# Routing two batches of the third group, instead of one, beside a half output projection

## What is computed

```python
x = x + tanh(g_xattn) * xattn(layernorm(x), ctx)        # 16 heads, latent dims, rope
n = layernorm(x).reshape(16 * 112, 512)
logits = n @ gate_w.T                                   # 64 experts
topv, topi = top_k(logits, 8)
W = zeros(N, 64).at[rows, topi].set(softmax(topv))
out = sum over experts e of (silu(gate_e(n)) * up_e(n)) * W[:, e] @ dp_w[e].T
out = out + sigmoid(n @ sh_gate1_w.T) * shared_mlp(n)
x = x + tanh(g_ffn) * out
```

## Time and profile before

| what | us |
|---|---|
| three executions | 1713.53, 1716.02, 1720.42 |
| median | 1716.02 |
| profiled execution, its own time | 1701.07 |
| its span, first to last instruction | 1699.2 |
| PE busy in the span | 1475.1 |
| DVE busy | 1138.6 |
| POOL busy | 994.1 |
| turning phase with routing of group 2 (g = 3) | 120.10 |
| half output pass, first transpose to last product | 996.24 to 1022.53 |

### The profile page before, as it was taken

The page is one execution under the profiler, slowest core; times in us unless marked ns, Lnnn a source line. Parts: engine busy times, 40 slices in busy tenths (PEclk is TensorE's granted clock), DMA queues, the critical chain, the costliest instruction groups (busy, mean ns, idle before and its releaser), DMA issues. The chain is left out here.

```text
span 1699.2 us, 24951 instructions
## 1 busy us (share of the span) xinstructions
PE 1475.1 (87%) x7674; PEld 1194.8 (70%) x7674; DVE 1138.6 (67%) x2438; ACT 690.5 (41%) x1579; POOL 994.1 (59%) x1003
## 2 busy tenths in 40 slices
PE   7998999998999999999999897827799888888684
PEld 5766887776887776787777676616688887787552
DVE  5777780687882588783489747233567766677697
ACT  2333770111771111771011535203566665666431
POOL 3654670376773277673277753245666776767388
PEclk9999999999999999999999999957999999999798
DMA  7897205555104655103655042435678888888796
GB/s 246 296 317 274 71 6 161 183 169 150 37 6 125 193 171 171 41 6 112 190 170 149 23 153 74 149 93 183 203 252 265 288 287 269 283 271 272 304 367 271
DMA packets 157228, 308.04 MB, mean 181 GB/s; under 512 B 31390, under 2 KB 66808, under 8 KB 155256
## 3 DMA queue, kind: packets, MB, share of 16 engines
q1 hardware_dynamic: 131752, 241.76, 42.7%
q0 software_dynamic: 25344, 64.69, 12.2%
HBM read 236.72 MB, written 71.80 MB: 182 GB/s over the span
## 5 line engine op out<-in xcount | busy, mean ns | idle before, releaser
L1738 POOL TENSOR_TENSOR q_rope<-q_rope,q_sin 128x448 f32<-128x448 f32 x192 | 217.7, 1162 | 152.6 <-DVE q_sin L1110 152.4
L1744 POOL TENSOR_TENSOR prob<-prob,row_inv 128x375 f32<-128x375 f32 x209 | 168.4, 812 | 112.9 <-DVE row_inv L1132 110.5
L1819 POOL DMA_INDIRECT parts<-y_sb,t_rows x140 | 142.4, 1017 | 114.0 <-ACT y_sb L1635 82.9
L1812 POOL DMA_INDIRECT x_g<-xn_dram,t_rows x140 | 156.1, 1115 | 47.1 <-issue 42.4
L1759 POOL DMA_INDIRECT table<-entry,pos_i x128 | 126.3, 987 | 89.3 <-DVE count L1220 58.8
L797 PE MATMUL bank<-q_rope,m_w 128*128 128x448 f32 x384 | 159.6, 552 | 13.7 <-DVE q_tl L1116 9.0
L1110 DVE TENSOR_TENSOR q_sin<-bank,sin_q 128x448 f32<-128x448 f32 (+1 forms) x256 | 157.9, 617 | 4.0
L1124 DVE TENSOR_REDUCE row_max<-bank 128x1 f32<-128x375 f32 x224 | 119.3, 534 | 35.5 <-PE bank L699 35.0
L1635 ACT ACTIVATE y_sb<-bank,t_rows 112x512 f32<-112x512 f32 (+2 forms) x140 | 91.4, 689 | 103.9 <-PE bank L699 59.7
L1498 ACT ACTIVATE prob<-bank,row_max 128x375 f32<-128x375 f32 x224 | 128.3, 573 | 9.7 <-DVE row_max L1124 9.1
L823 PE MATMUL bank<-ident,prob 128*125 128x128 f32 x672 | 115.4, 282 | 19.0 <-POOL prob L1744 8.7
(11 more groups left out here) (297 smaller groups left out, 4619.9 us busy)
## 6 DMA issues: line engine op xcount, KB each, us to landing
w_gu<-in_w_gu SPq DMA_DIRECT2D x64, 512.0 KB
p_in<-parts SPq DMA_DIRECT2D x14, 2048.0 KB, 10.4
w_dp<-in_w_dp SPq DMA_DIRECT2D x64, 256.0 KB
m_w<-m_dram SPq DMA_DIRECT2D x48, 192.0 KB
wq_s0h<-wq_dram SPq DMA_DIRECT2D x24, 256.0 KB
wq_s0l<-wq_dram SPq DMA_DIRECT2D x24, 256.0 KB
wq_s1h<-wq_dram SPq DMA_DIRECT2D x24, 256.0 KB
wq_s1l<-wq_dram SPq DMA_DIRECT2D x24, 256.0 KB
```

The lines of the kernel that those rows point to most:

```text
L1738: pool.tensor_tensor(o[:, c, :], o[:, c, :], q_sin[:, c, :], ALU.add).then_inc(s_radd, 1)
L1744: pool.tensor_tensor(prob[i][:], prob[i][:], row_inv[:, i:i + 1].to_broadcast([P, L]), ALU.mult)\
L1812: pool.indirect_dma_start(x_g[x % NXE][0:size, t, :], None, xn2_dram, bass.IndirectOffsetOnAxis(ap=t_rows[x % NROW][0:size, t, 0:1].bitcas ...
L1819: pool.indirect_dma_start(parts, bass.IndirectOffsetOnAxis(ap=t_rows[x % NROW][0:size, t, 1:2].bitcast(I32), axis=0), y_sb[x % NY][t][0:si ...
```

## The change

The third group leaves two batches over, 10 and 11, as groups 0 and 1 do. Batch 10's turn to scatters leave the fourth group's turning phase, and the two batches that stay there (8 and 9) take the slots that groups 0 and 1 use. In the half output pass both left-over batches are routed, with turn, router and rank before the heads 0, 2, 5 and 3, 6, 10, both in banks 3, 6 and 7 (before: batch 11 alone, before the heads 0, 2 and 6). Because both now use bank 6 for logits, batch 11's router waits until batch 10's mask is made.

```diff
-LEFT = (2, 2, 1, 0)
-START = {2: (0, 12, 20, 28), 1: (0, 9, 18, 28)}
+LEFT = (2, 2, 2, 0)
+START = (0, 12, 20, 28)
...
-    at = START[LEFT[g]][i]
+    at = START[i]
...
-    at = ({"turn": 0, "router": 2, "rank": 6},) if LEFT[p - 1] == 1 else \
+    at = ({"turn": 0, "router": 2, "rank": 5}, {"turn": 3, "router": 6, "rank": 10}) if p == NG - 1 else \
         ({"turn": 0, "router": 1, "rank": 3}, {"turn": 2, "router": 4, "rank": 7})
...
-        return (3, 6, 7) if LEFT[b // GB] == 1 else (0, 1 + b % 2, 3)
+        return (3, 6, 7) if b // GB == NG - 2 else (0, 1 + b % 2, 3)
...
-                    if 0 < b < B - GB and b not in left_over(b // GB):
+                    if 0 < b < B - GB and (b not in left_over(b // GB) or b == B - GB - 1):
                         pe.wait_ge(s_route, NR * (b - 1) + R_MASK)
```

## The result

The changed kernel took 1719.42 us (median of 20 executions) beside 1713.20 us of the kernel before (also 20, among them the three shown above). The ratio is 1.0043, with a 95% interval of 1.0025 to 1.0061: slower, by about 7.4 us, which is 0.43% of 1713.20 (the two medians themselves lie 6.2 us apart). The forecast was 1715.2 us, which is 0.8 us less than before instead of more. The profiled execution of the changed kernel had a span of 1720.3 us and a time of 1722.15 us.

The account below looks back on a forecast made before the run. DVE and PE were taken to bound the turning phase, PE and v_w loads the half output pass. Terms -1.57 (turning) and +0.8 (restart) gave -0.8 us, with the pass's 0.3 not added: 1715.2 us, range 1709.5 to 1721.5.

Parts of the forecast that it names:

- The turning phase: Fourth group's turning phase: heads 2 to 15 shorter by 1.57 us with two batches routed instead of three.
- a rival's condition: End of the turning phase: PE's clock stays up, 1.70 us more gain, time 1713.5 us; chance 0.2.
- The step that failed: Half output pass: the new scatters run beside the loads and count as nothing, at most 0.13 us.
- PE's steps: Half output pass: 1.37 us of added routing work on PE, lengthening the pass by 0.3 us, bounds 0.1 and 1.37.
- all three waits: Half output pass: PE's idle times before three heads, 1.24 us, put down to v_w loads; added work would shorten them.
- The restart: Attention behind the half output pass: POOL's sixteen scatters make ACT's exponentials late by 0.8 us, bounds 0 and 2.05.
- rival "slower": Restart: POOL's scatter row delays context copy and exponentials by 2.05 us, DVE by some 0.5; time 1717.0 us, chance 0.25.
- within 0.5%: Whole kernel: change too small to tell from none, 0.5% being 8.6 us; chance 0.88, against 0.06 faster and 0.06 slower.
- The case with every unknown cost at its upper bound: Whole kernel: no turning phase gain, restart 2.5 us and PE's added work 1.37 us; time 1719.9 us.
- no gain in the turning phase: Turning phase: the ring of engines, not routing, sets its length, so only 0.4 us gained; time 1716.4 us, chance 0.1.

Follow-up runs that it names:

- e3: Kernel before, with PE's products of batch 11's turn, router and rank made twice in the half output pass; ratio 1.0014, pass 27.88 us.
- e8: Changed kernel, with the scatters of both left-over batches moved behind the half output pass; ratio 1.0034, pass 26.91 us.
- e7: Kernel before, with batch 11's eight scatters moved behind the half output pass, one per attention tile; ratio 1.0012, pass 25.70 us.
- e16: Changed kernel, with six v_w pairs in the fourth group and both batches' scatters behind the pass; ratio 1.0007 to the kernel before, pass 25.28 us.
- e15: Kernel before, with six v_w pairs in the fourth group and batch 11's scatters behind the pass; ratio 0.9970, pass 23.67 us.
- e4: Changed kernel, with batch 11's eight scatters moved behind the pass, so eight stay in it; ratio 0.9998 to the kernel before, pass 28.53 us.
- e9: Kernel before, with eight additions of 128x448 on POOL behind batch 11's scatters; ratio 0.9990, pass 26.04 us.
- e14: Changed kernel, with one 128x448 addition on POOL behind each of the sixteen scatters; ratio 1.0049 to the kernel before, pass 26.64 us.
- e1: The changed kernel itself, run again for a second trace and set of times; ratio 1.0042 to the kernel before, pass 33.91 us.
- e2: Kernel before, with batch 11's eight scatters issued a second time into a table nobody reads; ratio 1.0057, pass 34.71 us.
- e6: Kernel before, with eight extra scatters of 16 rows each instead of 112; ratio 1.0041, pass 34.71 us.
- e11: Changed kernel, with six v_w pairs instead of four in the fourth group; ratio 1.0012 to the kernel before, pass 33.89 us.
- e13: Changed kernel, without the loads of v_w for heads 4 to 15 of the half output pass; pass 30.89 us, whole time not comparable.
- e5: Kernel before, with four of batch 11's scatters issued a second time, twelve in the pass; ratio 1.0019, pass 29.16 us.

## Why the prediction was wrong

**The turning phase was right, its size was low.** The predicted term was -1.57 us; the heads gained 2.0. The forecast had the clock at the stage's end fallen as before; in the profile of the changed kernel it stayed up there (2.49 us), which was a rival's condition, and fell in the stage of g = 2, which the change does not touch.

**The step that failed** is in the half output pass, whose whole term was +0.3 us and which took 7.9 more. It is this one: "The new scatters run beside the loads", with "I count them as nothing, at most 0.13". I priced the scatters by the one resource that I could read for them, the DMA engines' time and the rate of the loads. That reading was not false: with six pairs the loads moved 313 GB/s beside the scatters. But the cost doesn't lie there: the scatters cost by when the waits on PE's count end. The second eight in a dense row cost the pass 34.71 - 25.98 = 8.7 us when added alone, and without them the changed kernel has no loss. The half pass of before could not show it: with eight scatters POOL's row ends at 1018.2, 4.4 us ahead of the add. Passes 1 and 2 do hold sixteen scatters, and I didn't read them: in pass 2 of the kernel before they end at 550.8 and the pass at 563.9, so its end is in time, but SP learns of one head in the middle 0.9 us late. By its look that was the same thing, at a place where it costs nothing.

**PE's steps.** I took 0.3 us of a possible 1.37. The runs show 1.9 for twice batch 11's products (e3), and in pairs with and without the change 1.2 (e8 and e7), 1.6 (e16 and e15) and 2.5 (e4 and the kernel before). None of the added steps waited for its input, as predicted, and the stalls ahead of the `v_w` heads stayed (0.68 and 0.41 us after). So the work ahead of a load's wait was not absorbed, and even my upper bound was too low in three of the four; why it is exceeded no run shows. It may be that every later buffer is then freed later as well. The prediction also put all added steps before heads 3, 5 and 6, ahead of all three waits; the last, batch 11's rank, stands before head 10.

**The restart.** I predicted +0.8 us from POOL's row; the context copy came 1037.00 - 1030.86 = 6.1 us behind the add, against 28.56 - 22.56 = 6.0 before. So this term was nil, since the pass itself ended late. POOL's row ended about where I had it, 31.5 us behind the first transpose (30.9 predicted). e9 shows that a POOL row 3.6 us past the add costs nothing that can be measured; in e14 one 18 us past it goes with an attention of 94.7 us. The rival "slower" named the right engine's row of scatters, and a false path: not POOL's own next work, but PE's signals.

**Behind the pass.** The 3.5 us there weren't in any case of mine. In the changed kernel and in e1 the attention took 84.1 and 83.5 us, with the clock at 0.89. But in e2, where PE idles for 9.79 us before it, it took 79.1 at 0.96, less than before the change. So it is not shown that PE's long idle time costs these 3.5 us.

**What was luck.** The measured 1719.42 us lies in the range of 1709.5 to 1721.5, and the change stayed within 0.5%, to which the prediction gave 0.88. Both are owed to the width that the scatter of the medians had asked for. The case with every unknown cost at its upper bound came to 1719.9; that it is near is chance too, since it is made of a late restart (2.5, measured nil) and no gain in the turning phase (measured 2.0), and has no lag in it.

**What is shown and what is argued.** Shown: the scatters of the second batch cause the loss (e2, e4), per scatter and not per row or byte (e6), neither by starving PE of its loads (e11) nor through POOL being busy (e9), with the loads setting only the size (e13), and not when the pass is over before more than eight are out (e14, e4). Also shown: the wait's end goes by the start of the row and its number of scatters, not by PE. Argued: that it is the signal and not the product that is late. It rests on this schedule, on two heads that were seen 0.1 us apart (e5), on PE's rows without holes (e11), and on the trace's own times for PE, whose ends are modelled. The Trainium skill (Perfetto Trace Analysis, section "Per-instruction lifecycle: what the profiler-reported window actually captures") says that the propagation of a semaphore's update lies outside the window that the profile reports; 0.03 us of lag before and 6.94 after fit such a hidden part, and that section gives it no size. Open: what in a row of indirect transfers holds the signals up, why it lasts 1.42 to 1.44 us for each scatter beside loads and 1.25 without, and whether a spaced row of sixteen would be harmless, since in e14 only eight were out at the add.

## What to carry to other kernels

A long dense row of indirect transfers from POOL is not free because the DMA engines barely notice it: look at when the engines that wait for others' results start, beside the end of the instruction they wait for, and let such a row begin early before the stage's last wait (here by 1.43 us for each scatter, counted from the first). A new step's price should be bounded by each way in which it can touch the critical path, and where the trace before holds the same row at another place, that place is the thing to read. Where a stage is bound by loads, more buffers for it can be worth more than moving small work in and out of it: here six pairs gave 0.9945, and no place of the second batch gave anything.

## What the runs showed of the hardware

- While sixteen indirect transfers follow each other at 1.25 us, waits on PE's count end late on SP and DVE, growing over the row: 0.4, 2.6, 5.5 and 6.9 us for four heads. The profile shows the waiter's release as "remote", or not at all.
- The lateness ends 22.76 to 22.97 us behind the first of sixteen such transfers in five kernels, 17.21 us behind the first of twelve, and 11.40 to 11.47 us behind the first of eight in four; with no loads beside sixteen, 19.96 us.
- Eight scatters of 16 rows (0.85 us, 1.15 us apart) behind eight of 112 rows (0.94 us, 1.25 us apart) have the same effect as sixteen of 112 rows: pass 34.71 us in both. Each shows 32 packets in its queue, whatever its rows.
- Eight plain transfers from POOL behind eight scatters were issued in 4.27 us, with as many packets, and made no lag.
- PE's idleness of 7.95 us was followed by 1.2 GHz in the stretches from 1027 to 1037 and from 1044 to 1051, though PE was back at work at 1031.87. After 9.79 us of idleness in e2 the mean clock of the attention behind it was still 0.96.
